# Block 1 of a two-block kernel: the inverses of the softmax sums move from VectorE (a reciprocal) to GpSimd (a power of -1)

## The reference, cut to what matters

```python
x = layernorm(x + mixer0(x));  x = layernorm(x + ffn0(x))     # block 0
# block 1, attention; 16 heads of 64, 4 memory keys, causal
q, k = l2norm(q), l2norm(k)
dots = einsum('bhid,bhjd->bhij', q, k) * 10.0
dots = einsum('hg,bgij->bhij', W_pre_th, dots)                # heads are mixed
dots = where(causal, mask_value, dots)
vk   = top_k(dots, 64)[0][..., -1:]
dots = where(dots < vk, mask_value, dots)                     # the 64 largest stay
attn = softmax(dots)                                          # exp(dots - max) / sum
attn = einsum('hg,bgij->bhij', W_post_th, attn)               # heads are mixed back
out  = (attn @ v) * head_scale * sigmoid(x @ Wg + bg)
x = layernorm(x + out @ Wo);  x = layernorm(x + ffn1(x))
```

## Time and profile before

| | |
|---|---|
| median of three runs | 3660.3 us |
| span of the profiled execution | 3658.1 us |
| PE busy, matmuls / weight loads | 94% / 70% |
| DVE busy | 93% |
| ACT busy | 84% |
| POOL busy | 48% |
| chain that ended last | PE 64%, DVE 16%, ACT 14%, issue 3%, POOL 2% |

### The profile page before, as it was taken

The page is one execution under the profiler, slowest core; times in us unless marked ns, Lnnn a source line. Parts: engine busy times, 40 slices in busy tenths (PEclk is TensorE's granted clock), DMA queues, the critical chain, the costliest instruction groups (busy, mean ns, idle before and its releaser), DMA issues.

```text
span 3658.1 us, 79012 instructions
## 1 busy us (share of the span) xinstructions
PE 3438.4 (94%) x19551; PEld 2576.4 (70%) x19551; DVE 3392.9 (93%) x18541; ACT 3074.4 (84%) x10773; POOL 1743.1 (48%) x3672
## 2 busy tenths in 40 slices
PE   5999999996899999999999999999999999999997
PEld 4888888883566666666666666666666666666665
DVE  7898888854999999999999999999999999999994
ACT  6777777856799899899999899989988899989963
POOL 0000000003666666666666566666666666666653
PEclk7999999997899999999999999999999999999998
DMA  3000000002222222222222222222222222222220
GB/s 131 13 12 12 13 12 10 11 7 73 63 74 70 70 74 78 80 71 65 65 65 66 65 65 69 73 71 74 70 75 84 65 65 65 65 66 65 64 62 4
DMA packets 254141, 210.76 MB, mean 58 GB/s; under 512 B 78000, under 2 KB 234736, under 8 KB 252912
## 3 DMA queue, kind: packets, MB, share of 16 engines
q1 hardware_dynamic: 253680, 205.70, 18.0%
HBM read 93.97 MB, written 111.67 MB: 56 GB/s over the span
## 4 chain that ended last, share of the span: by engine, by line
PE 64%; DVE 16%; ACT 14%; issue 3%; POOL 2%; DMA 1%; SPq 0%; DVEq 0%; ACTq 0%; POOLq 0%
PE bank L363 11%; PE bank L221 7%; DVE W L1775 5%; PE bank L1383 5%; PE bank L1371 5%; PE bank L1356 4%; DVE last L1797 3%; PE bank L331 3%; PE bank L1414 3%; PE bank L453 3%; ACT SN L1567 3%; PE bank L195 3%; PE bank L1448 3%; PE bank L1428 2%; PE bank L1387 2%
## 5 line engine op out<-in xcount | busy, mean ns | idle before, releaser
L1775 DVE MATCH_REPLACE8 W<-last,W 128x130 f32<-128x130 f32 (+18 forms) x3456 | 871.0, 259 | 0.0
L1797 DVE MAX8 last<-W 128x8 f32<-128x130 f32 (+18 forms) x3456 | 761.9, 261 | 0.0
L1882 POOL TENSOR_SCALAR posts<-post,share 128x128 f32<-128x128 f32 x1024 | 366.5, 379 | 287.2 <-DVE share L1704 278.1
L894 DVE TENSOR_TENSOR_SCAN hs<-dA,dx 128x256 f32<-128x256 f32 x512 | 348.1, 680 | 86.6 <-issue 80.2
L1551 ACT ACTIVATE T<-T,peak 128x260 f32<-128x260 f32 (+15 forms) x1024 | 410.9, 409 | 4.2 <-POOL T L1933 3.3
L1567 ACT ACTIVATE SN<-bank,rq 128x260 f32<-128x260 f32 (+1 forms) x1024 | 357.8, 424 | 61.3 <-PE bank L1356 60.1
L1371 PE MATMUL bank<-T,pre 128*128 128x40 f32 (+15 forms) x1024 | 364.8, 439 | 15.0 <-ACT T L1575 10.1
L1383 PE MATMUL bank<-posts,T 128*128 128x128 f32 (+7 forms) x2048 | 310.2, 288 | 71.5 <-POOL posts L1882 63.4
L1933 POOL TENSOR_TENSOR T<-T,below 128x520 f32<-128x520 f32 (+12 forms) x416 | 360.5, 883 | 20.1 <-DVE below L1806 4.8
L1383 PEld LDWEIGHTS bank<-posts,T 128*128 128x128 f32 (+7 forms) x2048 | 247.2, 173 | 168.6 <-POOL posts L1882 93.8
L1898 POOL TENSOR_TENSOR T<-T,w_mask 128x32 f32<-128x32 f32 x512 | 141.0, 278 | 403.5 <-ACT T L1575 401.1
(11 more groups left out here) (244 smaller groups left out, 9584.0 us busy)
## 6 DMA issues: line engine op xcount, KB each, us to landing
scores_by_token<-SN SPq DMA_DIRECT2D x64, 520.0 KB, 2.6
scores_by_token<-SN SPq DMA_DIRECT2D x64, 396.0 KB, 3.2
scores_by_token<-SN SPq DMA_DIRECT2D x32, 780.0 KB, 3.3
scores_by_token<-SN SPq DMA_DIRECT2D x32, 264.0 KB, 2.6
scores_by_token<-SN SPq DMA_DIRECT2D x32, 260.0 KB, 2.0
T<-scores_by_token SPq DMA_DIRECT2D x32, 244.0 KB, 3.1
T<-scores_by_token SPq DMA_DIRECT2D x32, 228.0 KB, 3.3
T<-scores_by_token SPq DMA_DIRECT2D x32, 212.0 KB, 3.9
```

The source lines that it names most:

```text
L894: dve.tensor_tensor_scan(hs[j % NH][:], dA[j % ND][:], dx[b % 2][:], 0.0, ALU.mult, ALU.add).then_inc(scanned, 1)
L1775: dve.match_replace(both[:, s, at:to], best[n], both[:, s, at:to], LOWEST).then_inc(ranked, 1)
L1797: dve.max(best[n], both[:, s, at:to]).then_inc(ranked, 1)
L1882: pool.tensor_scalar(posts[(4 * k + j) % NP][:], post[:], share[k % 2][:, j:j + 1], 1.0, ALU.mult, ALU.mult).then_inc(posts_made, 1)
```

## The change

GpSimd makes `share` itself, by TENSOR_TENSOR with the operation pow: `total` to the power of a tile that holds -1 in all its 128 x 4 elements. DVE's 256 reciprocals and their two waits each are gone from its stream; POOL waits for the sums and for the buffer in their place, and between the power and the first of the four multiplications it waits for its own result. The beats are those of before: POOL's power stands where its wait for DVE stood.

```diff
@@ attention_phase
+    minus_one = room.sb("minus_one", [P, 4])
-    DVE_SHARE = (57, 80, 91, 99, 104, 118, 125, 136)
@@ vector
-        def share_out(k):
-            dve.wait_ge(e_made, 4 * (k + 1))
-            if k >= 2:
-                dve.wait_ge(posts_made, 4 * (k - 1))
-            dve.reciprocal(share[k % 2][:], total[k % 4][:]).then_inc(shared, 1)
@@
-                for i in range(QUADS):
-                    if (b := whose(p, t, DVE_SHARE[i])) is not None:
-                        share_out(QUADS * b + i)
@@ gpsimd
+        pool.memset(minus_one[:], -1.0)
@@
         def share_posts(k):
 
-            pool.wait_ge(shared, k + 1)
+            pool.wait_ge(e_made, 4 * (k + 1))
+            if k >= 2:
+                pool.wait_ge(posts_made, 4 * (k - 1))
+            pool.tensor_tensor(share[k % 2][:], total[k % 4][:], minus_one[:], ALU.pow).then_inc(shared, 1)
             if k >= NP // 4:
                 pool.wait_ge(back_mixed, 4 * (k + 1) - NP)
+            pool.wait_ge(shared, k + 1)
             for j in range(4):
                 pool.tensor_scalar(posts[(4 * k + j) % NP][:], post[:], share[k % 2][:, j:j + 1], 1.0, ALU.mult,
                                    ALU.mult).then_inc(posts_made, 1)
```

## The result

The changed kernel takes 3787.38 us (median of 4 runs, 3784.22 to 3789.11), the kernel before 3659.91 us (4 runs, 3659.46 to 3661.69). The ratio is 1.0351 with a 95% interval of 1.0336 to 1.0365: 127 us slower. The forecast was 3672 us with a range to 3716; the side is right, the size is not, and the time lies outside the range.

What follows compares the result with a forecast made beforehand. PE's loop through ACT, quad 7's exponentials, the inverse and `posts` was taken as the bound: 27 x 0.50 = +13.5 us, DVE's relief -1.9, the kernel's end +0.4, making +12 and 3672 us; range 3660 to 3716 us.

Steps and rivals of the forecast that it cites:

- The third rival: DVE's stream is the bound after all, so removing its reciprocals gains 21 us, to about 3640 us; chance 0.09.
- the 27 that the forecast put on PE's loop: Of 29.6 periods from 930 to 3436 us, 27 were taken as set by PE's loop and growing by 0.50 us each.
- The relief of DVE: DVE's stream without its reciprocals: nothing on PE-loop periods, gains only in three stretches where the chain lies on DVE; -1.9 us.
- The steps of quads 7 and 6: Delays of `posts` and drops by POOL's power at these two quads: 0.42 and 0.08, together 0.50 us a period.
- X - 0.08: Quad 7: `posts` start later by the power's duration X less 0.08 us, with nothing hiding it; 0.42 us a period.
- X - 0.42: Quad 6: the power delays quad 7's drops on POOL, adding X less 0.42 us where positive; 0.08 us a period.
- The price X: Duration of one power on POOL, shown by no row: taken as 0.5 us, between 0.198 and 1.281 us.
- the second rival: The power is dear, over 1 us, and the period grows by 2X - 0.5; at 1.3 us 3716 us; chance 0.22.
- for the quads before: Quads before 6: POOL's waits for DVE, 2.0 us each, cover the power up to about that length; no cost.
- by the same amount: PE's waits for `posts` at quad 7 grow from some 1.5 us by as much as the period between those `posts`.
- DVE's waits: DVE's wait for POOL's mask at the next sequence's start grows from 0.36 us to about 1.1 us and more.
- named signs of being wrong: Period not growing with X over 0.3 us, DVE's waits not growing, or quad 7's power starting over 0.2 us after its last exponential.

Runs made afterwards that it cites:

- e2: Kernel before with only quad 7's inverse made by POOL's power, the other seven by DVE's reciprocals; 3705.56 us, ratio 1.0138.
- e14: Kernel before with the inverses of quads 6 and 7 made by POOL's power, the rest by DVE's reciprocal; 3737.72 us, ratio 1.0207.
- e13: Kernel before with the inverses of quads 0 to 5 made by POOL's power, quads 6 and 7 by DVE's reciprocal; 3679.21 us, ratio 1.0044.
- e6: Changed kernel with 12 more 128x128 matmuls on TensorE before its wait for quad 7's posts; 3734.60 us, ratio 1.0200.
- e8: e7 with five more 128x128 matmuls on TensorE before the wait for quad 7's posts; 3706.14 us.
- e5: Changed kernel with quad 0's inverses back on DVE's reciprocal, quads 1 to 7 keeping the power; 3771.15 us, ratio 1.0298.
- e9: Instructions by themselves, no kernel: VectorE steps beside GpSimd resting, adding, scaling or at the power, then GpSimd alone; power 0.16 us a column over 0.39 us.
- e7: Kernel before with TensorE's mix waiting for each of the four posts as it comes to it, not all four first; 3704.26 us, ratio 1.0119.
- e12: e7 with one 128x16 scaling on GpSimd as padding ahead of the drops of quads 3 and 6; 3656.57 us, ratio 0.9993.

## Why the forecast was wrong

**The bound** was read rightly. PE's loop through the exponentials and the inverse of quad 7 sets the period of before: e2 delays only this hand-over and every period grows by what it adds. The third rival (DVE as the bound, 3640 us) is out, and with it what the occupancy suggested. The period grows throughout the phase, 31 times and not only in the 27 that the forecast put on PE's loop: 4 x 1.83 = 7 us more. The relief of DVE, -1.9 us in the sum, is seen in no run.

**The steps of quads 7 and 6** had the right form, X - 0.08 and X - 0.42 (e2 1.11, e14 0.72). The 0.08 us taken between two dependent steps of POOL is 0.17 here, and the four `posts`, taken as unchanged, are 0.09 us shorter. The two errors cancel, which is luck; the terms came out within some 0.1 us.

**The price X** was mis-sized: 0.5 taken, 1.03 measured, 1.21 beside DVE's step at quad 7 (the 0.2 us for such a neighbour was in the text and not in the sum). It was inside the bounds, which ended at 1.281. With the measured X the forecast's sum gives 27 x 1.74 = 47, less 1.9, plus about 1: some 3706 us. That is what the second rival said, and it is still 81 us short.

**The step that failed** is "for the quads before, POOL's waits for DVE (2.0 us each) cover the power". The 2.0 us are a mean over 129 waits. In the timeline of before POOL waits 3.4, 2.5 and 1.5 us ahead of `posts` of quads 0, 1 and 2, and not at all at 3 and 4, whose eight `posts` are one row in the section on the result. There the powers push `nd_rs` past PE's need: 0.55 us a period (e13, 17 us).

**The second step that failed** is the larger one, a term put at nothing: TensorE's clock. The stall at quad 7 was forecast to grow "by the same amount", and nothing was counted behind it. It grew from 1.5 to 3.15 us, the clock fell to 1.2 GHz there in each of 30 periods, and the first eight matmuls after it took 0.91 us more, with what follows them 1.6: 53 us (e6). The trace of before could have warned of the price. Four of its periods have a fall and are 86.3 to 86.4 us long, this one among them:
```profile
2329.41:2415.76 86.35, 82.95 (x501) 59.67 (x500) 84.26 (x533) 77.02 (x300) 53.85 (x115) 0.98 0.22 69
```
Of the place it says less: only one of the four falls is at the hand-over of quad 7 (near 2076 us), and three lie some 67 us behind it. The expectation of e8 took all the long periods for falls behind that stall, which they are not. A fifth long period (86.96 us) has no fall.

**DVE's waits** were to grow from 0.36 to 1.1 us and stayed at 0.43 (12.9 us over 30). This was one of the named signs of being wrong, and rightly: the slack was eaten by the holds, 3.4 us of DVE a period. That made DVE's stream as long as PE's loop (the chain is 25% on it), but hardly longer: e5 takes some 40% of the holds away (42 us of DVE) for 16 us, a part of which is the clock's.

**The account.** Quad 7 1.11, quad 6 0.72, quads 0 to 5 0.55, the clock 1.6: 3.98 of the 4.11 us by which the period grew. In runs: e6 stands 73 us over before, and 31 x (1.11 + 0.72 + 0.55) = 74; the clock is the other 53. Against the forecast's 3672 us that is 34 us for X, 17 for quads 0 to 5, 53 for the clock, 7 for the number of periods and 2 for the relief, 113 of 115. The 0.13 us left over goes with the holds, which is argued from e5 and not shown alone. The four long periods go with the clock.

## What to carry to other kernels

Price a moved instruction at each of its places, not at the mean wait of the engine that takes it: what counts is what stands behind it in order and who waits for that. Add to a longer stall of TensorE what its clock costs behind it, and try a few idle matmuls in the stall before concluding. When a fix on one engine makes the kernel slower, look for steps of VectorE, of two inputs above all, that now start just after one of GpSimd's. And read from the trace where in the period the clock falls before matmuls are added against it.

## What the hardware showed

- GpSimd's power costs 0.39 us and 0.16 us for each column (e9); four columns 1.02 us, where multiplication takes 0.20.
- GpSimd and VectorE shut each other out, instruction by instruction: 1.34 us for a scaling of 0.28 (e9), 0.99 for a step of 0.30 (e7, e12). MAX8 (0.41 us) was not touched. The Trainium skill says this in SBUF — State Buffer, Who interferes with whom: a VectorE instruction with two inputs in SBUF contends with a GpSimd instruction that reads it, and so does a scaling in a two-port mode; the loser is blocked for the whole instruction. The traces agree, though in which mode the scalings ran is not shown, with one exception that the page does not have: the power reads two inputs and did not lengthen VectorE's two-input step (0.41 against 0.42 us in e9). The other way round it was held, 1.21 us against 1.03, where it started 0.12 us after such a step.
- Whoever starts first wins, in every case looked at here, so 0.2 us of padding ahead of two drops was worth 48 us (e7 to e12), and an earlier TensorE cost 42.
